# The value product of an attention kernel as three 128-column products in one PSUM bank, in place of a 256- and a 128-column product over two banks

## The chip, the cores and the metric

The kernel runs on one NeuronCore of a Trainium2 chip. A core has a matrix engine (TensorE, PE in the rows, with its weight loads as PEld), VectorE (DVE), ScalarE (ACT), GpSimd (POOL) and a queue engine (SyncE, SP) that issues the transfers. The engines run side by side and wait for each other by semaphores. The metric is the device time of one execution in microseconds, as the median of several runs. A difference of under about 0.5% can't be told from no change here.

## What is computed

One transformer block over x of 8 sequences of 128 tokens and 256 channels, in float32, with 16 heads of 128, followed by a feed-forward stage with ternary weights. The part that matters here is attention:

```
ada = (timestep_embed @ ada_w + ada_b)[:, None, :]
x1 = _ln(x) * (1.0 + scale1) + shift1
qkv = (x1 @ qkv_w + qkv_b).reshape(Bc, Tc, 3, H, DH)
attn = jnp.einsum('bthd,bshd->bhts', q, k) * scale
attn = jax.nn.softmax(attn, axis=-1)
attn_out = jnp.einsum('bhts,bshd->bthd', attn, v).reshape(Bc, Tc, INNER)
attn_out = attn_out @ out_w + out_b
x = x + gate1 * attn_out
...
x = x + gate2 * (h @ ffn_w2 + ffn_b2)          # h = gelu(x2 @ ffn_w1 + ffn_b1)
return x + ternary_ffn(x)                      # relu^2, rms norm, ternary weights
```

## The kernel before

**Split operands.** TensorE multiplies in the format fp32r, which holds less than float32. So every operand is held as two fp32r tiles, a high part and a low part that is the rest, and a product is three: high by high, high by low, low by high, summed in PSUM. `split_mm` (lines 977 to 983) writes these three matmuls for each term. ScalarE makes the high parts out of PSUM (`biased_hi`, `hi_part`), VectorE the low parts (`biased_lo` at line 701, `plain_lo` at line 706): out of the same PSUM bank, it takes the value plus its bias minus the high part.

**Units.** The attention stage is 32 units, numbered i from 0 to 31: four groups of four heads (G), in each of them eight units j, a unit being one head of four sequences. The programs of all engines run over the units in one order, software pipelined: in unit i TensorE computes the scores of unit i (`scores`, 12 products of 128 columns through `split_mm`), transposes the probabilities of unit i-1 (line 1014), projects q and k for unit i+1, multiplies the head output of unit i-2 by the output weights (`out_product`), in four units of each eight also computes two blocks of v (`v_block`), and between these does the value product of unit i-1 (`pv`). Units 0 and 1 stand ahead of a loop over three groups, and the last six units behind it. The order on each engine is written by hand, as is every wait.

**The value product.** `pv(G, j)` waits for the low part of the probabilities (semaphore `p_l`) and for v. For each of the four sequences it takes the 128x128 block v_hi as the stationary operand against the high and the low half of p_split, laid out next to each other, as one product of 256 columns (line 1027), and then v_lo against the high half as one of 128 columns (line 1029), which adds to the first 128 columns of the 256. The result of four sequences takes 4 x 256 columns, that is the two banks of `pv_pair`: `pv_main` is the columns with two of the three terms, `pv_rest` those with the third.

**Its way out.** `o_hi_part` on ScalarE rounds pv_main plus bias to o_hi (semaphore `o_h`). `o_lo_part` on VectorE (lines 714 to 723) takes two instructions: pv_main plus bias minus o_hi into `pv_left` (the tile hbuf, line 720), then, behind a wait for it, pv_rest plus that into o_lo (line 723, semaphore `o_l`). In unit i VectorE does, in this order: the row maximum of the scores (line 779), its scaled copy (line 782), `o_lo_part` of unit i-2, the low part of the probabilities of unit i-1, the reciprocal of the row sums (line 788), the low parts of q and k, and then what the unit has besides. `out_product` of the same unit waits for `o_l`.

**After attention.** The last units also hold the first steps of what follows: transposes of the result (line 1147), the residual add (line 771), its normalisation (lines 654 to 672) and the modulation (line 685). Then come the feed-forward stage with `w1` and `w2` and the ternary stage, which ends the kernel.

Of the kernel before, what the change touches and what calls it, by code (L numbers as in the profile page):

```python
# [14 lines left out]
F32 = mybir.dt.float32  # L15
F32R = mybir.dt.float32r
BF16 = mybir.dt.bfloat16
ALU = mybir.AluOpType
# [3 lines left out]
P = 128  # L22
# [4 lines left out]
HG = 4  # L27
NG = H // HG
SQ = 4
NQ = B // SQ  # L30
TQ = SQ * P
HID = 1024
NC = HID // P
UG = NQ * HG
# [12 lines left out]
QB, KB, VB = NA, NA + H, NA + 2 * H  # L47
# [7 lines left out]
BQ, BK, BV, BS, BO, BY = 0, 1, 2, 3, 4, 6  # L55


def adaln_block(nc, x, cond, ada_w, ada_b, qkv_w, qkv_b, out_w, out_b, ffn_w1, ffn_b1, ffn_w2, ffn_b2,
                w_fc, w_proj, out):
    ctx = ExitStack()  # L60
    with ctx:
        def sb(name, shape, dt=F32):
            return ctx.enter_context(nc.sbuf_tensor(name, shape, dt))

        def sem(name):
            return ctx.enter_context(nc.semaphore(name))
# [24 lines left out]
        v_hi = sb("v_hi", [P, B, HG * P], F32R)  # L91
        v_lo = sb("v_lo", [P, B, HG * P], F32R)
# [5 lines left out]
        p_split = sb("p_split", [P, SQ, 2, P], F32R)  # L98
# [6 lines left out]
        hbuf = sb("hbuf", [P, 2, TQ])  # L105
# [13 lines left out]
        bias = sb("bias", [P, NBIAS])  # L119
# [22 lines left out]
        h2 = raw_qk[:, 0:2, :]  # L142
# [6 lines left out]
                (wo_hi[:, :, :].rearrange("p a b -> p (a b)"), wo_lo[:, :, :].rearrange("p a b -> p (a b)"))))  # L149
        w1T = wqk_hi[:, :, :].rearrange("p a b -> p (a b)")  # L150
        w2T = wqk_lo[:, :, :].rearrange("p a b -> p (a b)")
        pv_left = hbuf[:, 0, :]

        bank = [ctx.enter_context(nc.psum_tensor(f"bank{n}", [P, TQ], F32)) for n in range(BO)]
        pv_pair = ctx.enter_context(nc.psum_tensor("pv_pair", [P, 2 * TQ], F32))
        bank += [pv_pair[:, 0:TQ], pv_pair[:, TQ:2 * TQ]]
        bank += [ctx.enter_context(nc.psum_tensor(f"bank{n}", [P, TQ], F32)) for n in range(BY, 8)]

        pv_main, pv_rest = (pv_pair[:, :].rearrange("p (s x t) -> p s x t", s=SQ, x=2)[:, :, n, :] for n in range(2))


        cond_in, arow_in, bias_in, ada1_in, ada2_in = (
# [16 lines left out]
        q_mm, k_mm, s_mm, t_mm, v_mm, pv_mm, out_mm = (  # L179
            sem(n) for n in ("q_mm", "k_mm", "s_mm", "t_mm", "v_mm", "pv_mm", "out_mm"))  # L180
        q_h, k_h, exp_done, p_h, o_h, v_h = (sem(n) for n in ("q_h", "k_h", "exp_done", "p_h", "o_h", "v_h"))
        o_main = sem("o_main")
        max_done, nb_done, rinv_done, q_l, k_l, p_l, o_l, v_l, y_acc = (
            sem(n) for n in ("max_done", "nb_done", "rinv_done", "q_l", "k_l", "p_l", "o_l", "v_l", "y_acc"))
        norm_done = sem("norm_done")
# [55 lines left out]
        def head_output(i):  # L241

            return (q_hi, q_lo) if isinstance(i, int) and i == NU - 2 else (o_hi, o_lo)
# [57 lines left out]
        def _(pool):  # L301
# [92 lines left out]
            with pool.Fori(0, NG - 1) as G:  # L394
                for g, j, _, _ in group_units(G, range(2, UG + 2)):
                    unit(g, j)
                    if j == 0:
                        ternary_signs(G)
                    if j == 1:
                        ternary_values(G)  # L400
# [24 lines left out]
        def _(act):  # L425
# [32 lines left out]
            def biased_hi(hi, psum, at, ready, count, hi_sem):  # L458
                act.wait_ge(ready, count)
                act.nop(nofuse=True)  # L460
                nc.scalar.activation(hi, psum, ACT.Identity, bias=bias[:, bass.ds(at, 1)]).then_inc(hi_sem, 1)  # L461
# [7 lines left out]
                hi_part(p_split[:, :, 0, :], bank[BV][:, :].rearrange("p (s t) -> p s t", s=SQ), p_h)  # L469

            def o_hi_part(G, j):
                biased_hi(head_output(UG * G + j)[0][:, :].rearrange("p (s t) -> p s t", s=SQ), pv_main, HG * G + VB + j % HG, pv_mm, UG * G + j + 1, o_h)

            def before(G, j):
                return (G, j - 1) if j else (G - 1, UG - 1)
# [11 lines left out]
            def unit(G, j, vs, more, last=False):  # L487
# [50 lines left out]
                if not (isinstance(i, int) and i == 0):  # L538
                    o_hi_part(*before(G, j))
# [31 lines left out]

            modulate(2, SHIFT2, SCALE2, bank[0:2])
            o_hi_part(NG - 1, UG - 1)
            w2_hi_part(3)

# [70 lines left out]
        def _(dve):  # L646
# [29 lines left out]
            def modulate(e, shift, scale, src, between=None):  # L676

                quad = e % NQ
                dve.wait_ge(xt_done, e + 1)
                dve.wait_ge(ada_ready, 1 if e < NQ else 2)  # L680
                if e:
                    dve.wait_ge(xs_lo, KD * e)
                for s in range(SQ):
                    b = quad * SQ + s
                    m = nc.vector.tensor_scalar(xfull[:, 1, s * P:(s + 1) * P], src[1][:, s * P:(s + 1) * P],
                                                ada[:, scale + 1, b:b + 1], ada[:, shift + 1, b:b + 1], ALU.mult, ALU.add)
                m.then_inc(mod_d, 1)
                if between:
                    between()
                dve.wait_ge(mod_d, e + 1)  # L690
                split_lo(quad, KD * e)
# [19 lines left out]
            def p_lo_part(i):  # L711
                plain_lo(p_split[:, :, 1, :], bank[BV][:, :].rearrange("p (s t) -> p s t", s=SQ), p_split[:, :, 0, :], p_h, i + 1, p_l)

            def o_lo_part(G, j, left=pv_left):
                i = UG * G + j
                dve.wait_ge(o_h, i + 1)
                if not isinstance(i, int) or i:
                    dve.wait_ge(o_l, i)
                left, hi, lo = (t.rearrange("p (s t) -> p s t", s=SQ) for t in (left, *(o[:, :] for o in head_output(i))))
                nc.vector.scalar_tensor_tensor(out=left, in0=pv_main, scalar=bias[:, bass.ds(HG * G + VB + j % HG, 1)],  # L720
                                               in1=hi.bitcast(F32), op0=ALU.add, op1=ALU.subtract).then_inc(o_main, 1)
                dve.wait_ge(o_main, i + 1)
                nc.vector.tensor_tensor(lo, pv_rest, left, ALU.add).then_inc(o_l, 1)

            def before(G, j, n):
                return (G, j - n) if j >= n else (G - 1, UG + j - n)
# [33 lines left out]
            def ternary_compare(G, sign):  # L760
                dve.wait_ge(t_thrd, G + 1)
                w = t_bf[:, :].rearrange("p (s c) -> p s c", c=GROUP)
                dst = (t_up if sign > 0 else t_dn)[:, :].rearrange("p (s c) -> p s c", c=GROUP)
                nc.vector.scalar_tensor_tensor(out=dst, in0=w, scalar=float(sign), in1=t_thr[:, :].unsqueeze(2).broadcast_to([P, NS, GROUP]),
                                               op0=ALU.mult, op1=ALU.is_gt).then_inc(t_cmp, 1)
# [9 lines left out]
            def unit(G, j, vs, more, last=False):  # L775
# [7 lines left out]
                if not isinstance(i, int) or i >= 2:  # L783
                    o_lo_part(*before(G, j, 2))
# [60 lines left out]
            for g, j, vs, more in group_units(NG - 1, range(2, UG), last=True):  # L845
                unit(g, j, vs, more, last=True)
            o_lo_part(NG - 1, UG - 2)
            modulate(2, SHIFT2, SCALE2, bank[0:2], lambda: p_lo_part(NU - 1))
            o_lo_part(NG - 1, UG - 1, h2[:, 0, :])
            ternary_compare(NG - 1, -1)  # L850

            def h_lo_part(quad, c):
# [123 lines left out]
        def _(pe):  # L976
            def split_mm(dst, terms, start=True, stop=True):

                for n, (ah, al, bh, bl) in enumerate(terms):
                    nc.tensor.matmul(dst, ah, bh, start=start and n == 0, stop=False)  # L980
                    nc.tensor.matmul(dst, ah, bl, start=False, stop=False)  # L981
                    m = nc.tensor.matmul(dst, al, bh, start=False, stop=stop and n == len(terms) - 1)  # L982
                return m
# [33 lines left out]
            def pv(G, j):  # L1017
                a, quad = j % HG, j // HG
                pe.wait_ge(p_l, UG * G + j + 1)
                if isinstance(G, int) and UG * G + j == NU - 2:  # L1020
                    pe.wait_ge(o_l, NU - 2)
                pe.wait_ge(v_l, UG * G + SQ * (quad + 1))
                for s in range(SQ):
                    b, h = quad * SQ + s, slice(a * P, (a + 1) * P)
                    at = 2 * s * P

                    nc.tensor.matmul(pv_pair[:, at:at + 2 * P], v_hi[:, b, h], p_split[:, s, :, :].rearrange("p x t -> p (x t)"),  # L1027
                                     start=True, stop=False)
                    m = nc.tensor.matmul(pv_pair[:, at:at + P], v_lo[:, b, h], p_split[:, s, 0, :], start=False, stop=True)  # L1029
                m.then_inc(pv_mm, 1)  # L1030

            def out_product(G, j):
# [14 lines left out]
            def unit(G, j, vs, more, extra=None):  # L1047
# [13 lines left out]
                if known and i == NU - 1:  # L1061
                    transpose_xr(0, bank[0:2])
                    out_product(*before(G, j, 2))
                    pv(*before(G, j, 1))
                    pe.wait_ge(p_l, i)
                    transpose_p(i, j % 2)
                    pe.wait_ge(xrT_done, 1)
                    transpose_x(2, bank[0:2])
                    return
# [8 lines left out]
                if not known or i >= 1:  # L1078
                    pv(*before(G, j, 1))
# [7 lines left out]
            for k in range(KD):  # L1087
                m = nc.tensor.transpose(bank[7][:, k * B:(k + 1) * B], crow[:, k * P:(k + 1) * P], ident[0:B, 0:B])
# [244 lines left out]
```

## Time and profile before

| | us |
|---|---|
| median of 3 runs | 390.71 |
| lowest and highest | 390.7 and 392.43 |
| span of the profiled execution | 391.2 |

| engine | busy us | share of the span |
|---|---|---|
| PE | 367.8 | 94% |
| PEld | 319.5 | 82% |
| DVE | 288.0 | 74% |
| ACT | 237.0 | 61% |
| POOL | 129.7 | 33% |

Times in the rows are microseconds from the start of the profiled execution, except means, which are nanoseconds. Matmuls are pipelined: the end of one is modelled, and overlaps the start of the next, so that what a matmul costs in a dense stretch is the distance from its start to the start of the next one, and not its duration. Idle time of an engine is listed in front of the instruction that it waited for, with the engine and line that ended it.

### The profile page before, as it was taken

Reading aid. Unit: us, or ns where it says so; the run is one execution under the profiler, and the core shown is the slowest. Engines: PE = TensorE matmul, PEld = TensorE weight load, DVE = VectorE, ACT = ScalarE, POOL = GpSimd, SP = SyncE. Lnnn points to the kernel's source line nnn. Section 1 sums busy time; section 2 is a strip of 40 time slices with the busy share of each in tenths; the row PEclk is TensorE's granted clock in tenths of the full one; section 3 lists DMA queues with packets and bytes.
Section 4 is the critical chain, followed back from the end, with each engine's and each line's share of the span. In section 5 each row is a group of like instructions: output and inputs, shape, how many; then the busy total and the mean of one; then the engine's idle time right before and its main releaser. Section 6 shows DMA issues by size and latency. Waiting matters only on the chain. (4 is left out here: it accounts for less than half of the span.)

```text
span 391.2 us, 6260 instructions
## 1 busy us (share of the span) xinstructions
PE 367.8 (94%) x2096; PEld 319.5 (82%) x2096; DVE 288.0 (74%) x486; ACT 237.0 (61%) x582; POOL 129.7 (33%) x111
## 2 busy tenths in 40 slices
PE   2899999999999999999999999999889899996975
PEld 2789888888888888888888898889778787885855
DVE  5775569768776976866887667689988638797793
ACT  1464576665666566656676566775687358573751
POOL 1522224321542232272323144335423300162451
PEclk9999999999999999999999999999999999998995
DMA  7913031000303100030200012010000000000002
GB/s 231 358 61 108 1 109 54 2 0 3 108 0 107 54 0 0 0 107 29 78 0 0 0 26 83 0 55 1 2 0 1 2 0 2 0 1 2 8 19 80
DMA packets 11778, 16.53 MB, mean 42 GB/s; under 512 B 672, under 2 KB 7920, under 8 KB 11760
## 3 DMA queue, kind: packets, MB, share of 16 engines
q1 hardware_dynamic: 11760, 16.30, 12.6%
q8 instruction: 10, 0.16, 0.2%
q14 instruction: 8, 0.07, 0.1%
HBM read 15.25 MB, written 1.05 MB: 42 GB/s over the span
## 5 line engine op out<-in xcount | busy, mean ns | idle before, releaser
L345 POOL TENSOR_TENSOR prob<-prob,rinv 128x512 f32<-128x512 f32 x32 | 33.4, 1043 | 152.4 <-DVE rinv L788 152.4
L980 PE MATMUL bank<-x_hi,wqk_hi 128*128 128x512 f32 x128 | 54.4, 425 | 0.0
L982 PE MATMUL bank<-x_hi,wqk_lo 128*128 128x512 f32 x128 | 51.3, 401 | 0.0
L981 PE MATMUL bank<-x_lo,wqk_hi 128*128 128x512 f32 x128 | 51.1, 399 | 0.0
L706 DVE TENSOR_TENSOR v_lo<-bank,v_hi 128x512 fp32r<-128x512 f32 x30 | 20.7, 691 | 39.2 <-ACT v_hi L427 39.2
L493 ACT ACTIVATE prob<-bank,nbias 128x128 f32<-128x128 f32 x128 | 45.1, 370 | 4.1 <-DVE nbias L782 4.1
L427 ACT ACTIVATE p_split<-bank 128x512 fp32r<-128x512 f32 x32 | 19.1, 598 | 35.4 <-PE bank L1014 35.4
L461 ACT ACTIVATE o_hi<-pv_pair,bias 128x512 fp32r<-128x512 f32 x31 | 21.3, 688 | 24.3 <-PE pv_pair L1029 24.3
L982 PE MATMUL bank<-k_hi,q_lo 128*128 128x128 f32 x128 | 35.4, 276 | 0.0
L417 POOL TENSOR_TENSOR raw_qk<-raw_qk 128x512 f32<-128x512 f32 x13 | 18.4, 1415 | 50.7 <-ACT raw_qk L622 50.4
L981 PE MATMUL bank<-k_lo,q_hi 128*128 128x128 f32 x128 | 35.2, 275 | 0.0
L980 PE MATMUL bank<-k_hi,q_hi 128*128 128x128 f32 x128 | 34.3, 268 | 0.0
L1027 PE MATMUL pv_pair<-p_split,v_hi 128*128 128x256 f32 x128 | 31.4, 323 | 0.4 <-DVE xr L771 0.2
L427 ACT ACTIVATE v_hi<-bank 128x512 fp32r<-128x512 f32 x30 | 17.9, 596 | 22.7 <-PE bank L982 22.5
L779 DVE TENSOR_REDUCE negmax<-bank 128x4 f32<-128x512 f32 x32 | 22.1, 690 | 11.0 <-PE bank L982 11.0
L982 PEld LDWEIGHTS bank<-x_hi,wqk_lo 128*128 128x128 f32 x128 | 24.8, 193 | 5.9
L701 DVE SCALAR_TENSOR_TENSOR k_lo<-bank,bias,k_hi 128x512 fp32r<-128x512 f32 x32 | 24.0, 749 | 7.0 <-ACT k_hi L461 7.0
L981 PEld LDWEIGHTS bank<-x_lo,wqk_hi 128*128 128x128 f32 x128 | 24.9, 195 | 4.4
L1029 PE MATMUL pv_pair<-p_split,v_lo 128*128 128x128 f32 x128 | 28.5, 222 | 0.0
L980 PEld LDWEIGHTS bank<-x_hi,wqk_hi 128*128 128x128 f32 x128 | 24.9, 194 | 4.1
L701 DVE SCALAR_TENSOR_TENSOR q_lo<-bank,bias,q_hi 128x512 fp32r<-128x512 f32 x32 | 24.0, 751 | 5.0 <-ACT q_hi L461 3.4
L461 ACT ACTIVATE k_hi<-bank,bias 128x512 fp32r<-128x512 f32 x32 | 22.2, 692 | 8.6 <-PE bank L982 8.6
(206 smaller groups left out, 1086.9 us busy)
## 6 DMA issues: line engine op xcount, KB each, us to landing
raw_qk<-in_L_cond_qkv_w_dram SPq DMA_DIRECT2D x8, 512.0 KB, 4.9
raw_v<-in_L_cond_qkv_w_dram SPq DMA_DIRECT2D x4, 512.0 KB, 3.8
raw_o<-in_L_cond_out_w_dram SPq DMA_DIRECT2D x4, 512.0 KB, 3.6
xt<-in_x_dram SPq DMA_DIRECT2D x2, 512.0 KB, 5.0
xr<-in_L_cond_ada_w_dram SPq DMA_DIRECT2D x1, 1024.0 KB, 10.2
raw_w<-in_L_cond_ffn_w_dram SPq DMA_DIRECT2D x2, 512.0 KB, 7.6
t_raw<-in_L_ffn_W_fc_dram SPq DMA_DIRECT2D x4, 256.0 KB, 3.8
t_raw<-in_L_ffn_W_proj_dram SPq DMA_DIRECT2D x4, 256.0 KB, 3.9
```

Source lines behind the costliest of these rows:

```text
L345: nc.gpsimd.tensor_tensor(e, e, rinv[:, j % 2, :].unsqueeze(2).broadcast_to([P, SQ, P]), ALU.mult).then_inc(norm_done, 1)
L427: nc.scalar.activation(hi, raw, ACT.Copy).then_inc(hi_sem, 1)
L461: nc.scalar.activation(hi, psum, ACT.Identity, bias=bias[:, bass.ds(at, 1)]).then_inc(hi_sem, 1)
L493: e = nc.scalar.activation(prob[:, j % 2, s, :], bank[BS][:, s * P:(s + 1) * P], ACT.Exp, bias=nbias[:, j % 2, s:s + 1], scale=SCALE, accu ...
L701: nc.vector.scalar_tensor_tensor(out=lo[:, :], in0=psum[:, :], scalar=bias[:, bass.ds(at, 1)], in1=hi[:, :].bitcast(F32), op0=ALU.add, op1 ...
L706: nc.vector.tensor_tensor(lo, psum, hi.bitcast(F32), ALU.subtract).then_inc(lo_sem, 1)
L779: nc.vector.tensor_reduce(negmax[:, j % 2, :], bank[BS][:, :].rearrange("p (s t) -> p s t", s=SQ), axis=AX.X, op=ALU.max, negate=True).the ...
L980: nc.tensor.matmul(dst, ah, bh, start=start and n == 0, stop=False)
L981: nc.tensor.matmul(dst, ah, bl, start=False, stop=False)
L982: m = nc.tensor.matmul(dst, al, bh, start=False, stop=stop and n == len(terms) - 1)
L1027: nc.tensor.matmul(pv_pair[:, at:at + 2 * P], v_hi[:, b, h], p_split[:, s, :, :].rearrange("p x t -> p (x t)"), start=True, stop=False)
L1029: m = nc.tensor.matmul(pv_pair[:, at:at + P], v_lo[:, b, h], p_split[:, s, 0, :], start=False, stop=True)
```

## The change

The value product is written with `split_mm`, as the scores are: for each sequence v_hi by p_hi, v_hi by p_lo and v_lo by p_hi, each of 128 columns, all three into the same 128 columns of one bank. `pv_pair`, its two halves and the buffer `pv_left` are gone, the banks 4 and 5 are separate ones, and `o_lo_part` is one call of `biased_lo`, with one instruction. The waits for `o_main` and for the preceding `o_l` go with the second instruction. Nothing else changes.

```diff
-        pv_pair = ctx.enter_context(nc.psum_tensor("pv_pair", [P, 2 * TQ], F32))
-        bank += [pv_pair[:, 0:TQ], pv_pair[:, TQ:2 * TQ]]
...
-        pv_main, pv_rest = (pv_pair[:, :].rearrange("p (s x t) -> p s x t", s=SQ, x=2)[:, :, n, :] for n in range(2))
+        bank = [ctx.enter_context(nc.psum_tensor(f"bank{n}", [P, TQ], F32)) for n in range(8)]
...
             def o_hi_part(G, j):
-                biased_hi(head_output(UG * G + j)[0][:, :].rearrange("p (s t) -> p s t", s=SQ), pv_main, HG * G + VB + j % HG, pv_mm, UG * G + j + 1, o_h)
+                biased_hi(head_output(UG * G + j)[0][:, :], bank[BO][:, :], HG * G + VB + j % HG, pv_mm, UG * G + j + 1, o_h)
...
-            def o_lo_part(G, j, left=pv_left):
-                i = UG * G + j
-                dve.wait_ge(o_h, i + 1)
-                if not isinstance(i, int) or i:
-                    dve.wait_ge(o_l, i)
-                left, hi, lo = (t.rearrange("p (s t) -> p s t", s=SQ) for t in (left, *(o[:, :] for o in head_output(i))))
-                nc.vector.scalar_tensor_tensor(out=left, in0=pv_main, scalar=bias[:, bass.ds(HG * G + VB + j % HG, 1)],
-                                               in1=hi.bitcast(F32), op0=ALU.add, op1=ALU.subtract).then_inc(o_main, 1)
-                dve.wait_ge(o_main, i + 1)
-                nc.vector.tensor_tensor(lo, pv_rest, left, ALU.add).then_inc(o_l, 1)
+            def o_lo_part(G, j):
+                hi, lo = head_output(UG * G + j)
+                biased_lo(lo, bank[BO], HG * G + VB + j % HG, hi, o_h, UG * G + j + 1, o_l)
...
-                    at = 2 * s * P
-
-                    nc.tensor.matmul(pv_pair[:, at:at + 2 * P], v_hi[:, b, h], p_split[:, s, :, :].rearrange("p x t -> p (x t)"),
-                                     start=True, stop=False)
-                    m = nc.tensor.matmul(pv_pair[:, at:at + P], v_lo[:, b, h], p_split[:, s, 0, :], start=False, stop=True)
+                    m = split_mm(bank[BO][:, s * P:(s + 1) * P], [(v_hi[:, b, h], v_lo[:, b, h], p_split[:, s, 0, :], p_split[:, s, 1, :])])
```

How instructions stand in a row, first on TensorE in the loop: the value product of unit i-1, between the output product (o_hi, o_lo against wo) and the scores of the next unit. Before:

```order
L982 MATMUL bank<-o_hi,wo_lo 128x512
L1027 MATMUL pv_pair<-p_split,v_hi 128x256
L1029 MATMUL pv_pair<-p_split,v_lo 128x128
L1027 MATMUL pv_pair<-p_split,v_hi 128x256
L1029 MATMUL pv_pair<-p_split,v_lo 128x128
...
L980 MATMUL bank<-k_hi,q_hi 128x128
L981 MATMUL bank<-k_lo,q_hi 128x128
```

In the changed kernel `split_mm` has the lines 966 to 968:

```order
L968 MATMUL bank<-o_hi,wo_lo 128x512
L966 MATMUL bank<-p_split,v_hi 128x128
L967 MATMUL bank<-p_split,v_hi 128x128
L968 MATMUL bank<-p_split,v_lo 128x128
L966 MATMUL bank<-p_split,v_hi 128x128
L967 MATMUL bank<-p_split,v_hi 128x128
L968 MATMUL bank<-p_split,v_lo 128x128
...
L966 MATMUL bank<-k_hi,q_hi 128x128
L967 MATMUL bank<-k_lo,q_hi 128x128
```

Eight matmuls have become twelve, in the same place; each brings a weight load of its own. The second place is VectorE in unit 31, the last one, from the row maximum to the modulation (xfull) that follows attention. Before:

```order
L779 TENSOR_REDUCE negmax<-bank 128x4
L782 TENSOR_SCALAR nbias<-negmax 128x4
L720 SCALAR_TENSOR_TENSOR hbuf<-pv_pair,bias,o_hi 128x512
L723 TENSOR_TENSOR o_lo<-pv_pair,hbuf 128x512
L706 TENSOR_TENSOR p_split<-bank,p_split 128x4x128
L788 RECIPROCAL rinv<-rowsum 128x4
L672 TENSOR_SCALAR raw_qk<-xr,mv,rstd 128x256 x4
L720 SCALAR_TENSOR_TENSOR hbuf<-pv_pair,bias,q_hi 128x512
L723 TENSOR_TENSOR q_lo<-pv_pair,hbuf 128x512
L685 TENSOR_SCALAR xfull<-bank,ada 128x128 x4
```

In the changed kernel:

```order
L765 TENSOR_REDUCE negmax<-bank 128x4
L768 TENSOR_SCALAR nbias<-negmax 128x4
L694 SCALAR_TENSOR_TENSOR o_lo<-bank,bias,o_hi 128x512
L699 TENSOR_TENSOR p_split<-bank,p_split 128x4x128
L774 RECIPROCAL rinv<-rowsum 128x4
L665 TENSOR_SCALAR raw_qk<-xr,mv,rstd 128x256 x4
L694 SCALAR_TENSOR_TENSOR q_lo<-bank,bias,q_hi 128x512
L678 TENSOR_SCALAR xfull<-bank,ada 128x128 x4
```

The second instruction of each o_lo is gone (the pair on q_lo is that of unit 30, whose head output lies in q_hi and q_lo), and all that follows it on VectorE has moved up by one place; no instruction has changed its order.

## Rows read from the trace of the kernel before

**Rows 1.** The page: its head, and busy us (share of the span) xinstructions.
```profile
span 391.2 us, 6260 instructions
...
PE 367.8 (94%) x2096; PEld 319.5 (82%) x2096; DVE 288.0 (74%) x486; ACT 237.0 (61%) x582; POOL 129.7 (33%) x111
```
**Rows 2.** Busy time by stretch (PE, PEld, DVE, ACT, POOL; PEclk, DMA share, GB/s).
```profile
43.00:275.00 232.00, 232.00 (x1372) 204.04 (x1371) 172.84 (x292) 148.96 (x406) 81.62 (x65) 1.00 0.11 34
275.00:291.00 16.00, 13.52 (x90) 11.22 (x88) 14.85 (x34) 12.03 (x31) 5.88 (x6) 1.00 0.00 1
...
338.00:391.00 53.00, 42.04 (x230) 36.65 (x228) 40.31 (x49) 28.14 (x52) 21.55 (x16) 0.88 0.06 20
```
**Rows 3.** Groups by line, 43 to 275 us, PE (busy us, mean ns, idle before).
```profile
L982 PE MATMUL bank<-k_hi,q_lo 128*128 128x128 f32 x116 | 32.0, 276 | 0.0
...
L1027 PE MATMUL pv_pair<-p_split,v_hi 128*128 128x256 f32 x116 | 28.3, 322 | 0.0
```
**Rows 4.** Groups by line, 43 to 275 us, DVE.
```profile
L720 DVE SCALAR_TENSOR_TENSOR hbuf<-pv_pair,bias,o_hi 128x512 f32<-128x512 f32 x29 | 21.7, 749 | 0.6
...
L723 DVE TENSOR_TENSOR o_lo<-pv_pair,hbuf 128x512 fp32r<-128x512 f32 x29 | 20.0, 691 | 1.0
```
**Rows 5.** Timeline, PE, a unit with v blocks (start, duration, engine, line, xcount).
```profile
108.30 0.28 PE L1027 MATMUL pv_pair<-p_split,v_hi 128*128 128x256 f32 x1
...
109.17 0.45 PE L980 MATMUL bank<-wv_hi,x_hi 128*128 128x512 f32 x1
...
110.60 0.22 PE L980 MATMUL bank<-k_hi,q_hi 128*128 128x128 f32 x1
...
111.89 0.62 PE L1014 MATMUL bank<-ident,prob 128*128 128x128 f32 x4
```
**Rows 6.** Timeline, PE, scores that follow a value product directly.
```profile
101.01 0.28 PE L980 MATMUL bank<-k_hi,q_hi 128*128 128x128 f32 x1
...
102.35 0.63 PE L1014 MATMUL bank<-ident,prob 128*128 128x128 f32 x4
```
**Rows 7.** Timeline, PE, eight 128-column products with bf16 operands.
```profile
324.12 0.62 PE L1213 MATMUL bank<-ident_bf,t_w 128*128 128x128 bf16 x8
324.55 0.48 PE L980 MATMUL bank<-x_hi,w_hi 128*128 128x512 f32 x1
```
**Rows 8.** The page: costliest groups, ScalarE on two banks and on one.
```profile
L461 ACT ACTIVATE o_hi<-pv_pair,bias 128x512 fp32r<-128x512 f32 x31 | 21.3, 688 | 24.3 <-PE pv_pair L1029 24.3
...
L461 ACT ACTIVATE k_hi<-bank,bias 128x512 fp32r<-128x512 f32 x32 | 22.2, 692 | 8.6 <-PE bank L982 8.6
```
**Rows 9.** Timeline, DVE, two instructions of the form that the change leaves.
```profile
269.36 0.75 DVE L701 SCALAR_TENSOR_TENSOR q_lo<-bank,bias,q_hi 128x512 fp32r<-128x512 f32 x1
270.02 0.74 DVE L701 SCALAR_TENSOR_TENSOR k_lo<-bank,bias,k_hi 128x512 fp32r<-128x512 f32 x1
```
**Rows 10.** Timeline, DVE, units 31 and after ([idle before <-releaser]).
```profile
281.69 0.75 DVE L720 SCALAR_TENSOR_TENSOR hbuf<-pv_pair,bias,o_hi 128x512 f32<-128x512 f32 x1
282.48 0.69 DVE L723 TENSOR_TENSOR o_lo<-pv_pair,hbuf 128x512 fp32r<-128x512 f32 x1
283.08 0.68 DVE L706 TENSOR_TENSOR p_split<-bank,p_split 128x512 fp32r<-128x512 f32 x1
...
286.59 0.75 DVE L720 SCALAR_TENSOR_TENSOR hbuf<-pv_pair,bias,q_hi 128x512 f32<-128x512 f32 x1 [0.75 <-ACT q_hi L461]
```
**Rows 11.** Timeline, PE, where it waits near the end of attention.
```profile
278.37 0.39 PE L1027 MATMUL pv_pair<-p_split,v_hi 128*128 128x256 f32 x1 [0.22 <-DVE xr L771]
...
283.22 0.50 PE L980 MATMUL bank<-o_hi,wo_hi 128*128 128x512 f32 x1 [1.04 <-DVE o_lo L723]
...
288.12 0.50 PE L980 MATMUL bank<-q_hi,wo_hi 128*128 128x512 f32 x1 [1.03 <-DVE q_lo L723]
...
289.99 0.39 PE L1027 MATMUL pv_pair<-p_split,v_hi 128*128 128x256 f32 x1 [0.20 <-DVE p_split L706]
...
291.19 0.50 PE L980 MATMUL bank<-x_hi,w_hi 128*128 128x512 f32 x1
```

More of the change, by code:

```diff
@@ L151, in adaln_block @@
         w2T = wqk_lo[:, :, :].rearrange("p a b -> p (a b)")
-        pv_left = hbuf[:, 0, :]
-        bank = [ctx.enter_context(nc.psum_tensor(f"bank{n}", [P, TQ], F32)) for n in range(BO)]
-        pv_pair = ctx.enter_context(nc.psum_tensor("pv_pair", [P, 2 * TQ], F32))
-        bank += [pv_pair[:, 0:TQ], pv_pair[:, TQ:2 * TQ]]
-        bank += [ctx.enter_context(nc.psum_tensor(f"bank{n}", [P, TQ], F32)) for n in range(BY, 8)]
-        pv_main, pv_rest = (pv_pair[:, :].rearrange("p (s x t) -> p s x t", s=SQ, x=2)[:, :, n, :] for n in range(2))
+        bank = [ctx.enter_context(nc.psum_tensor(f"bank{n}", [P, TQ], F32)) for n in range(8)]
         cond_in, arow_in, bias_in, ada1_in, ada2_in = (
@@ L181, in adaln_block @@
         q_h, k_h, exp_done, p_h, o_h, v_h = (sem(n) for n in ("q_h", "k_h", "exp_done", "p_h", "o_h", "v_h"))
-        o_main = sem("o_main")
         max_done, nb_done, rinv_done, q_l, k_l, p_l, o_l, v_l, y_acc = (
@@ L848, in _ @@
             modulate(2, SHIFT2, SCALE2, bank[0:2], lambda: p_lo_part(NU - 1))
-            o_lo_part(NG - 1, UG - 1, h2[:, 0, :])
+            o_lo_part(NG - 1, UG - 1)
             ternary_compare(NG - 1, -1)
```

## Prediction

> **What bounds the kernel now.** The head of the page comes first [rows 1]: TensorE is busy for 94% of the span, VectorE for 74%. That is an average, so the next view is the busy time by stretch [rows 2]. From 43 to 275 us, which holds 29 of the 32 value products (116 of the 256-column matmuls, four to a block, [rows 3]), TensorE is busy for 232.00 of 232.00 us at the full granted clock, and VectorE for 172.84. From 275 to 291 us it is the other way round: VectorE 14.85 of 16, TensorE 13.52. In the last stretch neither is full, and the work there (the ternary stage) isn't touched.
>
> The groups by line say the same from the side of the waits: in the long stretch the idle time before the value product and before the scores is 0.0 [rows 3]. VectorE is never late for TensorE there. Only near the end of attention does TensorE stand and wait for VectorE, four times, and two of these waits, of 1.04 and 1.03 us, are for the second instruction of o_lo [rows 11]. So the change takes work from an engine that has slack in 232 of 391 us, and the question is what it adds to the one that has none.
>
> **What a value product costs on TensorE.** A busy PE says nothing of its price, since the rows overlap; starts do. Before, a block of four sequences runs from 108.30 to 109.17, when the next product starts: 0.87 us for 8 matmuls [rows 5], about 0.11 us for each, whether it has 256 or 128 columns. The new block is 12 matmuls of 128 columns through the same helper as the scores, with operands of the same type and size, of which the first two share their stationary operand. So the scores are the price of the new block. After a 512-column product, as the value product also comes, the 12 matmuls of the scores run from 110.60 to 111.89: 1.29 us [rows 5]. After a value product, whose last matmul is a short one, they run from 101.01 to 102.35: 1.34 us [rows 6]. I take 1.29, since a value product follows a 512-column one in the order of both kernels, and keep 1.34 for the upper end. The price of a block is 1.29 - 0.87 = **0.42 us**, up to 0.47.
>
> That it is the number of weight loads that costs and not the columns can be seen twice. Both forms stream 4 x 384 columns, and yet 12 matmuls take half as long again as 8. And with bf16 operands eight products of 128 columns take 324.55 - 324.12 = 0.43 us, 0.054 each [rows 7], half of the 0.11 of the fp32r ones: neither the columns nor the issue of instructions holds the latter. There are as many loads as matmuls, 2096 of each [rows 1], so a load isn't left out where two products in a row have the same weights.
>
> The Trainium skill, "TensorE: Matmul & The Clock Gate", section "Back-to-back issue gap", gives for an isolated stream 134 cycles at 128 columns and 262 at 256, some 56 and 109 ns; by it a block would cost 4 x (109 + 56) = 0.66 us before and 12 x 56 = 0.67 after, that is nothing more. The same section's sustained 81 ns for 128 columns would make the new block 0.97 us and the difference 0.10 us a unit, 3 us in all. Its section on LDWEIGHTS, 128 columns / 1.2 = 107 ns, is the one near the rows here, and four loads more by it are 0.43 us.
>
> **TensorE in the long stretch.** 29 blocks x 0.42 = **+12.2 us** (29 x 0.47 = 13.6 at most). All of it is on the path, since there is no idle time in front of any of them.
>
> **What VectorE saves.** Before, o_lo is two instructions, 749 and 691 ns [rows 4]; from the start of the first to the start of what follows the second it takes 283.08 - 281.69 = 1.39 us [rows 10]. After, it is one of the form of q_lo, whose successor starts 270.02 - 269.36 = 0.66 us later [rows 9]. So 0.73 us a unit go, 23 us of busy time over 32 units. In the long stretch they go into VectorE's idle time and bring nothing: TensorE waits for no VectorE result there. The output on one bank in place of two costs ScalarE the same: 688 ns for o_hi, 692 for k_hi out of one bank [rows 8]. Nothing moves past a queue, no wait is added, and no transfer or GpSimd instruction changes: no cost.
>
> **The end of attention.** Here the 0.73 us counts, against three more blocks (29, 30, 31) of 0.42. I walk it relative to the shift that the 29 blocks have made. Block 29 waits for the residual add (278.37, [rows 11]). VectorE comes to this add some 0.7 us earlier but then has to wait for TensorE's transposes, so the block starts only 0.2 us earlier, and with its 0.42 the scores behind it start 0.1 to 0.2 us later than before. Then o_lo of unit 29 is ready about 0.6 us earlier (one instruction instead of two, from a start 0.1 us later), and the output product, which waited 1.04 us for it, starts at about -0.6. Block 30 takes that to -0.2. The next o_hi is bound by ScalarE and comes 0.1 us later, so o_lo starts at 286.7 and is ready at 287.4 instead of 288.1 [rows 10, 11]: the output product starts at -0.65. Block 31 waits behind the modulation for p_lo, which is earlier by the same amount, and with its 0.42 the feed-forward stage starts at about **-0.3 us** against 291.19. From -1 to +0.5 seems possible, as three waits change owner here.
>
> **Behind it.** The feed-forward and ternary stages have the same instructions. What can change is where the low clock falls: from 338 us on the mean granted clock is 0.88 of full [rows 2], and TensorE isn't full there. I count 0, with 1 us to either side.
>
> **Sum.** 12.2 - 0.3 = +11.9 us on the span of 391.2, which gives 403.1. The median of the runs, 390.7, is 0.5 below the profiled span, so I forecast 402.6 us, 3% slower. From the terms' ends: 390.7 + 11.9 - 0.7 - 1 = 400.9 and 390.7 + 13.6 + 0.5 + 1 = 405.8.
>
> **Rivals.** (A) Not slower: the price is in the columns, or the second load of v_hi comes for free, so that a block still costs 0.87 us. What speaks for it: the array streams the same 1536 columns. Then only the end of attention changes: the two waits of 1.04 and 1.03 us for o_lo lose up to 0.7 each, 390.7 - 1.4 = 389.3 us. If short products even ran at the bf16 pace of 0.054 us, a block would be 12 x 0.054 = 0.65 us, 29 x 0.22 = 6.4 us less, near 383 us. It decides from a spacing of below 0.073 us a matmul (0.87 / 12). Against it: the scores' 0.11 us in every unit. The skill's table of isolated gaps, named above, is this rival. (B) A smaller loss: TensorE's unbroken busy time hides short waits for VectorE of under 0.2 us that the overlap of the rows covers, and VectorE's freed 0.73 us takes them away. With 0.1 to 0.2 us in each of 29 units, 3 to 6 us come back: 396.6 to 399.7 us. Against it: the starts inside and around the blocks are evenly spaced. (C) A larger loss: in the half of the units without v blocks the new block stands directly in front of the scores, and 12 + 12 + 4 short products follow each other where it was 8 + 12 + 4. If TensorE's supply of instructions falls behind there by 0.22 us, the shortest idle time that it has in these rows [rows 11], 15 units pay 3.3 us more: 405.9 us. Against it: 12 + 4 in a row run at 0.11 us without a gap.
>
> **Chances.** Forecast (400 to 405.5) 0.84; A 0.05, of which 0.03 at 389 and 0.02 below; B 0.06; C 0.05. Taken together the range is 400.0 to 405.4 us. The bound of 0.5% lies at 388.8 and 392.7 us: faster 0.02, the same 0.03, slower 0.95.
>
> **What would show it.** In the changed kernel's rows: starts of the value product's matmuls 0.11 us apart and a block of 1.29 us (A: 0.87 or less); loads and matmuls 2096 + 128 = 2224 of each; VectorE busy for some 22 us less, near 266, and TensorE still without idle time to the end of unit 28; the waits of 1.04 and 1.03 us for o_lo down to 0.3 to 0.6. If the loop's units grow by clearly less than 0.42 us with blocks of 1.29, it is B, if there are gaps inside a run of short products, C. The forecast is wrong above all if the scores are no fair model of the new block: their operands come from tiles of 512 columns, those of the value product from v_hi with 4096 and from the interleaved halves of p_split.

## The result and the profile after

| | before | changed |
|---|---|---|
| median us | 390.7 (4 runs) | 402.92 (4 runs) |
| lowest and highest | 390.65 and 392.43 | 402.21 and 404.13 |
| ratio, 95% interval | | 1.0295 [1.0258, 1.0332] |
| span of the profiled execution | 391.2 | 400.7 |

The change makes the kernel 12.2 us slower, against a forecast of 11.9. The spans of the two profiled executions differ by 9.5 us only; that gap is taken up below.

The head of the page, and busy time by stretch (PE, PEld, DVE, ACT, POOL, then PEclk), of the changed kernel. They answer to [rows 1] and [rows 2]:

```profile
span 400.7 us, 6452 instructions
...
PE 378.9 (95%) x2224; PEld 331.2 (83%) x2224; DVE 268.3 (67%) x454; ACT 236.8 (59%) x582; POOL 129.5 (32%) x111
```
```profile
43.00:285.00 242.00, 242.00 (x1473) 214.26 (x1472) 154.21 (x262) 148.33 (x406) 80.23 (x64) 1.00 0.10 33
285.00:301.00 16.00, 15.20 (x103) 12.73 (x102) 13.00 (x30) 11.45 (x29) 5.82 (x6) 1.00 0.00 0
```

TensorE has 128 matmuls and 128 loads more and is still busy without a gap from 43 to 285 us. VectorE has 32 instructions and 19.7 us less to do (288.0 to 268.3), all of which it now spends waiting. The value product on TensorE in a unit without v blocks, and its start behind a v block, which answer to [rows 5] and [rows 6]:

```profile
100.83 0.22 PE L966 MATMUL bank<-p_split,v_hi 128*128 128x128 f32 x1
100.89 0.28 PE L967 MATMUL bank<-p_split,v_hi 128*128 128x128 f32 x1
101.00 0.27 PE L968 MATMUL bank<-p_split,v_lo 128*128 128x128 f32 x1
...
102.12 0.28 PE L966 MATMUL bank<-k_hi,q_hi 128*128 128x128 f32 x1
...
103.46 0.40 PE L1000 MATMUL bank<-ident,prob 128*128 128x128 f32 x2
```
```profile
109.41 0.22 PE L966 MATMUL bank<-p_split,v_hi 128*128 128x128 f32 x1
...
110.70 0.45 PE L966 MATMUL bank<-wv_hi,x_hi 128*128 128x512 f32 x1
```

A block takes 102.12 - 100.83 = 1.29 us, or 110.70 - 109.41 = 1.29, where it took 0.87. The scores behind it take 103.46 - 102.12 = 1.34, as before. The weight loads (PEld) start 0.11 us apart as well, each at about the time at which the product ahead of its own starts:

```profile
100.84 0.19 PEld L967 LDWEIGHTS bank<-p_split,v_hi 128*128 128x128 f32 x1
100.95 0.19 PEld L968 LDWEIGHTS bank<-p_split,v_lo 128*128 128x128 f32 x1
```

To measure the whole long stretch free of what happens at either end, take the start of the scores of unit 2 and of unit 30. In the kernel before:

```profile
45.23 0.22 PE L980 MATMUL bank<-k_hi,q_hi 128*128 128x128 f32 x1
...
271.15 0.28 PE L980 MATMUL bank<-k_hi,q_hi 128*128 128x128 f32 x1
```

In the changed one:

```profile
43.43 0.22 PE L966 MATMUL bank<-k_hi,q_hi 128*128 128x128 f32 x1
...
281.10 0.28 PE L966 MATMUL bank<-k_hi,q_hi 128*128 128x128 f32 x1
```

225.92 us have become 237.67: +11.75, or 0.42 for each of the 28 blocks between (units 2 to 29, with the value products of units 1 to 28). These two starts are the yardstick for the experiments too; below they are "the 28 units".

### The profile page after: what moved, and what is told of

Same layout as the page of the kernel before. It is cut to its first block and busy times, and to the rows that moved or that the text cites. A ratio compares the mean times of both kernels' runs of the same rounds, so it can differ in the third digit from the quotient of the medians.

```text
span 400.7 us, 6452 instructions
## 1 busy us (share of the span) xinstructions
PE 378.9 (95%) x2224; PEld 331.2 (83%) x2224; DVE 268.3 (67%) x454; ACT 236.8 (59%) x582; POOL 129.5 (32%) x111
## 3 DMA queue, kind: packets, MB, share of 16 engines
q1 hardware_dynamic: 11760, 16.30, 12.2%
## 5 line engine op out<-in xcount | busy, mean ns | idle before, releaser
L966 PE MATMUL bank<-x_hi,wqk_hi 128*128 128x512 f32 x128 | 53.2, 415 | 0.0
L699 DVE TENSOR_TENSOR v_lo<-bank,v_hi 128x512 fp32r<-128x512 f32 x32 | 22.1, 691 | 45.8 <-ACT v_hi L420 45.8
L968 PE MATMUL bank<-x_hi,wqk_lo 128*128 128x512 f32 x128 | 50.3, 393 | 0.0
L967 PE MATMUL bank<-x_lo,wqk_hi 128*128 128x512 f32 x128 | 49.8, 389 | 0.0
L454 ACT ACTIVATE o_hi<-bank,bias 128x512 fp32r<-128x512 f32 x31 | 21.3, 688 | 36.6 <-PE bank L968 36.6
L968 PE MATMUL bank<-p_split,v_lo 128*128 128x128 f32 x128 | 35.3, 276 | 0.0
L967 PE MATMUL bank<-p_split,v_hi 128*128 128x128 f32 x128 | 35.2, 275 | 0.0
L966 PE MATMUL bank<-p_split,v_hi 128*128 128x128 f32 x128 | 33.6, 262 | 0.2 <-DVE p_split L699 0.2
L420 ACT ACTIVATE v_hi<-bank 128x512 fp32r<-128x512 f32 x32 | 19.2, 599 | 23.3 <-PE bank L968 23.2
```

The lines of the kernel that those rows point to most:

```text
L420: nc.scalar.activation(hi, raw, ACT.Copy).then_inc(hi_sem, 1)
L699: nc.vector.tensor_tensor(lo, psum, hi.bitcast(F32), ALU.subtract).then_inc(lo_sem, 1)
```

## The experiments

The theory is that of the prediction: an fp32r product of 128 or of 256 columns costs what its weight load costs, 0.11 us, so the price is in the number of products; VectorE's relief counts at the end of attention only. The rivals are that the adding of three products into one bank costs, that columns cost, that VectorE's lateness was hidden in every unit, and that the cost can be had back by another order. Every kernel is compared with the kernel before on the same chip; its median was 392.03 (29 runs) in the comparison with e1, e2, e3 and e6, and 391.08 (17 runs) in that with the others. The expectations give their times from a kernel before of 390.7, so what can be held against them is the difference.

| kernel | products in a block, columns in all | banks, o_lo instructions | median us | ratio to before | 28 units us | block us |
|---|---|---|---|---|---|---|
| before | 8, 1536 | 2, 2 | 390.7 | 1 | 225.92 | 0.87 |
| changed | 12, 1536 | 1, 1 | 402.92 | 1.0295 [1.0258, 1.0332] | 237.67 | 1.29 |
| e1 | 12, 1536 | 2, 2 | 404.82 | 1.0333 [1.0296, 1.0369] | 237.68 | 1.29 |
| e2 | 8, 1536 | 2, 1 | 390.63 | 0.9971 [0.9946, 0.9995] | 225.71 | 0.87 |
| e3 | 8, 2048 | 2, 2 | 392.65 | 1.0021 [0.9999, 1.0044] | 226.50 | 0.95 |
| e6 | 8, 1024 | 1, 1 | 390.71 | 0.997 [0.9945, 0.9996] | 225.19 | 0.84 |
| changed, again | 12, 1536 | 1, 1 | 403.43 | 1.0302 [1.0272, 1.0333] | 237.67 | 1.29 |
| e5 | 12, 1536 | 1, 1 | 404.77 | 1.0348 [1.0318, 1.0378] | 238.21 | 2.68 with the output product |
| e7 | 8, in two units 12 | 2, 2 and 1, 1 | 391.02 | 0.999 [0.9966, 1.0014] | 226.00 | 0.87, in two units 1.29 |

The start of what follows a block is drawn up to 0.06 us earlier or later by whether a wide or a narrow product stands last, so the 28 units are the better measure of a price than one block.

### e1: twelve products, but two banks and two VectorE instructions

```diff
-                    nc.tensor.matmul(pv_pair[:, at:at + 2 * P], v_hi[:, b, h], p_split[:, s, :, :].rearrange("p x t -> p (x t)"),
-                                     start=True, stop=False)
+                    nc.tensor.matmul(pv_pair[:, at + P:at + 2 * P], v_hi[:, b, h], p_split[:, s, 1, :], start=True, stop=True)
+                    nc.tensor.matmul(pv_pair[:, at:at + P], v_hi[:, b, h], p_split[:, s, 0, :], start=True, stop=False)
```

> The kernel before, with its 256-column product cut into two of 128 columns (p_lo into its half of the pair first, then p_hi); both banks, both VectorE instructions of o_lo and all waits stay. Theory (a weight load costs 0.11 us whether its product has 128 or 256 columns): blocks of 1.29 us, 29 x 0.42 = +12.2 us, and since VectorE is not relieved the last three blocks cost too, +0.5 to +1.3: 403.4 to 404.2 us. Rival (the three terms in one bank, adding to the same 128 columns, are what costs): blocks stay near 0.87 us and the time near 391 us.

Measured: 404.82 us, 12.8 more than before, where the expectation had 12.7 to 13.5 (403.4 to 404.2 less 390.7). The 28 units take 237.68 us, to 0.01 those of the changed kernel. So the whole cost in the long stretch comes from cutting the wide product in two, and the single bank has no part in it. At the end of attention TensorE waits for VectorE as in [rows 11]:

```profile
295.02 0.50 PE L980 MATMUL bank<-o_hi,wo_hi 128*128 128x512 f32 x1 [1.04 <-DVE o_lo L723]
...
300.32 0.50 PE L980 MATMUL bank<-q_hi,wo_hi 128*128 128x512 f32 x1 [1.02 <-DVE q_lo L723]
```

From the scores of unit 30 (282.76) to the first product of the feed-forward stage (303.58) it is 20.82 us, in the changed kernel 300.80 - 281.10 = 19.70. The difference, 1.12 us, is what the changed kernel gains by its shorter o_lo.

### e2: one VectorE instruction, TensorE untouched

```diff
...
-                nc.vector.scalar_tensor_tensor(out=left, in0=pv_main, scalar=bias[:, bass.ds(HG * G + VB + j % HG, 1)],
-                                               in1=hi.bitcast(F32), op0=ALU.add, op1=ALU.subtract).then_inc(o_main, 1)
-                dve.wait_ge(o_main, i + 1)
-                nc.vector.tensor_tensor(lo, pv_rest, left, ALU.add).then_inc(o_l, 1)
+                nc.vector.scalar_tensor_tensor(out=lo, in0=pv_main, scalar=bias[:, bass.ds(HG * G + VB + j % HG, 1)],
+                                               in1=hi.bitcast(F32), op0=ALU.add, op1=ALU.subtract).then_inc(o_l, 1)
```

> The kernel before, with TensorE untouched and o_lo as one VectorE instruction: the second one, which adds v_hi by p_lo, is left out, so that term is missing from the output. It prices VectorE's relief by itself. Theory (the relief counts at the end of attention alone): the waits of 1.04 and 1.03 us shrink to 0.3 to 0.4, 389.0 to 390.0 us. Rival (TensorE's unbroken busy time hides short waits for VectorE in every unit): 3 to 6 us less, 385 to 388 us.

Measured: 390.63 us against 392.03, 0.9971 [0.9946, 0.9995]; the 1.4 us less are in what was expected (0.7 to 1.7), though the time itself isn't, since the kernel before took 392.03 there. The 28 units shrink by 0.21 us of 225.92, where the rival asked for 3 to 6. Of the 0.21, 0.18 are hidden waits of the rival's kind after all: three units (4, 12 and 20) of the kernel before last 6.86 us, the others of their form 6.80, as all of them do here. No such wait stands on TensorE's matmul rows, but one stands on its weight loads, in front of the output product, in the kernel before:

```profile
65.99 0.19 PEld L980 LDWEIGHTS bank<-o_hi,wo_hi 128*128 128x128 f32 x1 [0.20 <-DVE o_lo L723]
```

The page shows VectorE at 268.8 us in place of 288.0: 19 us of work taken from an engine, and in the trace about 1 us of time, 0.21 in the 28 units, 0.54 at the end of attention, where 20.04 us become 19.50, and 0.25 behind it. TensorE's waits there, as in [rows 11], with VectorE's relief:

```profile
280.48 0.50 PE L976 MATMUL bank<-o_hi,wo_hi 128*128 128x512 f32 x1 [0.31 <-DVE o_lo L718]
283.91 1.07 PE L1102 MATMUL bank<-ident,raw_qk 128*128 128x128 f32 x8 [0.46 <-DVE raw_qk L672]
285.23 0.50 PE L976 MATMUL bank<-q_hi,wo_hi 128*128 128x512 f32 x1 [0.25 <-DVE q_lo L718]
...
288.64 0.50 PE L976 MATMUL bank<-x_hi,w_hi 128*128 128x512 f32 x1 [0.40 <-DVE x_lo L696]
```

The two waits of 1.04 and 1.03 us did shrink to 0.31 and 0.25. But two others have come up, 0.46 for the normalised x and 0.40 for the low part of the modulated one, which were hidden behind them. That is why 1.5 us less of waiting for o_lo is worth 0.54. In the changed kernel, whose blocks are longer, less of these two shows (the transposes of the normalised x start 0.21 us later behind those ahead of them than before, and no listed wait is for x_lo), and the same relief is worth the 1.12 us found with e1.

### e3 and e6: eight products, all wide or all narrow

e3, in the kernel before:

```diff
-                    m = nc.tensor.matmul(pv_pair[:, at:at + P], v_lo[:, b, h], p_split[:, s, 0, :], start=False, stop=True)
+                    m = nc.tensor.matmul(pv_pair[:, at:at + 2 * P], v_lo[:, b, h], p_split[:, s, :, :].rearrange("p x t -> p (x t)"),
+                                         start=False, stop=True)
```

> The kernel before, with v_lo against both halves of p, so that all eight products of a block have 256 columns (2048 columns in place of 1536; a fourth term is added to the output). Theory (loads set the price): a block of 0.87 to 0.92 us, 391 to 392.3 us. Rival (columns set it): 0.87 x 2048 / 1536 = 1.16 us a block, +8.4 us, 399 us.

e6, in the changed kernel:

```diff
-                    m = split_mm(bank[BO][:, s * P:(s + 1) * P], [(v_hi[:, b, h], v_lo[:, b, h], p_split[:, s, 0, :], p_split[:, s, 1, :])])
+                    at = bank[BO][:, s * P:(s + 1) * P]
+                    nc.tensor.matmul(at, v_hi[:, b, h], p_split[:, s, 0, :], start=True, stop=False)
+                    m = nc.tensor.matmul(at, v_hi[:, b, h], p_split[:, s, 1, :], start=False, stop=True)
```

> The changed kernel without its third term (v_lo by p_hi is left out of the output): eight products of 128 columns a block, 1024 columns, one bank, one VectorE instruction. Theory (loads set the price): a block of 0.85 us, as before the change with half as many columns again, 389 to 390 us. Rival (columns): 0.87 x 1024 / 1536 = 0.58 us a block, -8.4 us, 381 us. A spacing between means that the weights of two products in a row, which are the same here in all of them, are in part loaded for free.

Measured: 392.65 and 390.71 us, that is 0.6 more and 1.3 less than before, near the theory and far from the rival (+8.4 and -8.4). A block of e3 takes 0.95 us, a little above the 0.87 to 0.92 expected. Starts of the products in e3, all of 256 columns:

```profile
97.64 0.28 PE L1027 MATMUL pv_pair<-p_split,v_hi 128*128 128x256 f32 x1
97.76 0.28 PE L1029 MATMUL pv_pair<-p_split,v_lo 128*128 128x256 f32 x1
97.88 0.28 PE L1027 MATMUL pv_pair<-p_split,v_hi 128*128 128x256 f32 x1
...
98.59 0.22 PE L980 MATMUL bank<-k_hi,q_hi 128*128 128x128 f32 x1
```

And in e6, all of 128:

```profile
98.25 0.28 PE L1013 MATMUL bank<-p_split,v_hi 128*128 128x128 f32 x1
98.36 0.27 PE L1012 MATMUL bank<-p_split,v_hi 128*128 128x128 f32 x1
98.47 0.27 PE L1013 MATMUL bank<-p_split,v_hi 128*128 128x128 f32 x1
...
99.03 0.28 PE L966 MATMUL bank<-k_hi,q_hi 128*128 128x128 f32 x1
```

0.12 us from start to start with 256 columns, 0.11 with 128. Over the 28 units, twice as many columns (e3 against e6) cost 226.50 - 225.19 = 1.31 us, 0.05 a unit, of which 0.21 in all is VectorE's, by e2; four products more of the same size (the changed kernel against e6) cost 237.67 - 225.19 = 12.48 us, 0.45 a unit, 0.11 for each. Columns up to 256 are nearly free, products aren't. The rival by columns, with 399 and 381 us, is out. In e6 the two products of a sequence have the same weights throughout, and keep the spacing of 0.11: nothing is saved on a load that repeats the one before.

What these runs show is a price for each product. That it is the price of its weight load is the reading that fits them, with the loads' starts 0.11 us apart; no run changes the load and leaves the product. One row of the kernel before fits it too, 16 products of only 8 columns (their weights are plain float32):

```profile
33.69 1.84 PE L1097 MATMUL bank<-condT,xr 128*128 128x8 f32 x16
35.39 0.31 PE L980 MATMUL bank<-k_hi,q_hi 128*128 128x128 f32 x1
```

From the first to what follows it is 1.70 us, 0.106 for each.

### e5: the short products between long ones

If loads are the price and a 512-column product takes twice the 0.11 us at which loads follow each other (0.227), the spare time could be under the long products. The edit, in the changed kernel, in the units without v blocks:

```diff
...
+                for k in range(6):
+                    c, x, y, n = long[k]
+                    w = (wo_hi, wo_lo)[x][:, a, c * P:(c + 1) * P]
+                    ml = nc.tensor.matmul(bank[BY + c][:, :], w, y[:, :], start=a == 0 and n == 0, stop=a == HG - 1 and n == 2)
+                    for s, m3 in short[2 * k:2 * k + 2]:
...
+                        ms_ = nc.tensor.matmul(bank[BO][:, s * P:(s + 1) * P], (v_hi, v_hi, v_lo)[m3][:, b, h],
+                                               p_split[:, s, (0, 1, 0)[m3], :], start=m3 == 0, stop=m3 == 2)
```

> The changed kernel, where in the units without v blocks the twelve 128-column products of the value product stand between the six 512-column ones of the output product: one long, two short, one long, two short, and so on; both waits come ahead of the first. Nothing else changes. Theory (a load runs under the one product ahead of it and no further): a pair of short ones after a long one costs two loads more, as before, so the joined block takes 6 x 0.227 + 12 x 0.11 = 2.7 us and the time is the changed kernel's, within 0.5%. Rival (loads run ahead under a long product by more than one): columns set the pace, 6 x 0.227 + 12 x 0.056 = 2.03 us, 0.6 us less in each of some 14 units, 394 us.

Measured: 404.77 us, 1.0348 [1.0318, 1.0378], against 403.43 us, 1.0302 [1.0272, 1.0333], for the changed kernel run beside it, for which this was expected:

> The changed kernel once more, on the same chip as the two that follow. Ratio to the kernel before 1.029 to 1.033.

The joined block, L1029 being the long products:

```profile
99.44 0.39 PE L1029 MATMUL bank<-o_hi,wo_hi 128*128 128x512 f32 x1
99.67 0.33 PE L1032 MATMUL bank<-p_split,v_hi 128*128 128x128 f32 x2
99.83 0.45 PE L1029 MATMUL bank<-o_lo,wo_hi 128*128 128x512 f32 x1
100.12 0.22 PE L1032 MATMUL bank<-p_split,v_lo 128*128 128x128 f32 x1
100.18 0.27 PE L1032 MATMUL bank<-p_split,v_hi 128*128 128x128 f32 x1
100.29 0.45 PE L1029 MATMUL bank<-o_hi,wo_lo 128*128 128x512 f32 x1
...
102.12 0.28 PE L966 MATMUL bank<-k_hi,q_hi 128*128 128x128 f32 x1
```

And its loads:

```profile
99.89 0.19 PEld L1032 LDWEIGHTS bank<-p_split,v_lo 128*128 128x128 f32 x1
100.12 0.19 PEld L1032 LDWEIGHTS bank<-p_split,v_hi 128*128 128x128 f32 x1
```

One long and two short ones take 100.29 - 99.83 = 0.46 us, and the block 102.12 - 99.44 = 2.68, where six long ones and then twelve short ones take 6 x 0.227 + 1.29 = 2.65. The loads fit this: that of the first short product is done at 100.08, under the long one, and that of the second doesn't start before the first short product does, at 100.12. So in these runs a load is hidden under no more than the one product ahead of it, and the spare time under a long product can't be collected for two short ones. The time is even a little worse: the 28 units take 0.54 us more than the changed kernel's, and the end of attention 0.72 more (20.42 against 19.70). There, in unit 29, the output product ends only with the joined block, and VectorE, which adds it up, starts later by that; the delay goes on to the residual add and from there to the value product in unit 30, which isn't joined:

```profile
281.52 1.41 DVE L721 SCALAR_TENSOR_TENSOR yT<-bank,bias,yT 128x512 f32<-128x512 f32 x2 [0.98 <-PE bank L1029]
289.21 0.33 PE L966 MATMUL bank<-p_split,v_hi 128*128 128x128 f32 x1 [0.74 <-DVE xr L757]
```

The rival, 394 us, is out.

### e7: the changed form where TensorE waits, and only there

The result of e2 and the changed kernel's waits suggest a version between the two: pairs in units 0 to 28 and 31, one bank in 29 and 30.

```diff
+        def one_bank(i):
+            return isinstance(i, int) and i in (NU - 3, NU - 2)
...
+                if one_bank(i):
+                    hi, lo = head_output(i)
+                    return biased_lo(lo, bank[BO], HG * G + VB + j % HG, hi, o_h, i + 1, o_l)
...
+                    if one_bank(UG * G + j):
+                        m = split_mm(bank[BO][:, s * P:(s + 1) * P], [(v_hi[:, b, h], v_lo[:, b, h], p_split[:, s, 0, :], p_split[:, s, 1, :])])
+                        continue
```

> The kernel before, with the changed form (three 128-column products into one bank, one VectorE instruction) in units 29 and 30 alone, where TensorE waits for o_lo. Theory: the two waits of 1.04 and 1.03 us shrink by 0.7 each, two blocks cost 0.42 more, net -0.4 to -0.8 us against the kernel before, 0.1 to 0.2% less, which the ratio can hardly tell from 1; the waits in the profile tell. Rival (the relief is worth nothing at the end either, since another wait takes its place): +0.4 to +0.8 us.

Measured: 391.02 us against 391.08, 0.999 [0.9966, 1.0014]. The expected gain is missed. Its waits:

```profile
282.29 0.50 PE L988 MATMUL bank<-o_hi,wo_hi 128*128 128x512 f32 x1 [0.30 <-DVE o_lo L706]
...
287.05 0.50 PE L988 MATMUL bank<-q_hi,wo_hi 128*128 128x512 f32 x1 [0.25 <-DVE q_lo L706]
...
290.46 0.50 PE L988 MATMUL bank<-x_hi,w_hi 128*128 128x512 f32 x1 [0.40 <-DVE x_lo L701]
```

The waits for o_lo went as expected, 1.5 us of them. Two blocks took 0.84 of that. The transposes of the normalised x start 0.22 us later behind those ahead of them than before, and at the entry of the feed-forward stage, where the listed wait is 0.40 for x_lo, the last block and what follows it take 1.54 us in place of 1.20. From the scores of unit 30 (270.54) to that entry it is 19.92 us, 0.12 less than before: theory and rival each had half of it. No version here that computes all three terms beats the kernel before by more than a measurement can tell.

## Why the prediction was right, step by step

**The bound.** TensorE without a gap through the attention stage, VectorE with slack: confirmed after the change by the busy times above and by e2, where 19 us less work on VectorE moved the 28 units by 0.21 us. "VectorE is never late for TensorE there" was a little too strong: it is, by 0.06 us in three units. Nor is the end of attention the only other place where TensorE waits for it: the trace before has 1.21 us for v_lo at 310.63, in the feed-forward stage, and 3.9 and 2.9 us in all for two low parts in the ternary stage. None of these is for o_lo.

**The price of a block.** 0.42 us taken from the scores, 0.42 measured, in the changed kernel and in e1. The step that could have failed was to take the scores as the model of a block with other operands; they were a fair one. That the price is by products and not by columns, which the prediction read from two places in the trace, is shown by e3 and e6; that it is the loads' stays a reading. The table of isolated spacings in the Trainium skill ("TensorE: Matmul & The Clock Gate", section "Back-to-back issue gap"), which would have made the change free on TensorE, doesn't hold for this stream: it gives 56 ns for 128 columns, and e6 and the changed kernel show 0.11 us.

**The sum.** 28 blocks of +11.75 in all and the first one, whose distance from its start to the scores of unit 2 grew from 2.30 to 2.73 us, make 12.2, the number of the sum.

**The end of attention.** Forecast -0.3 against the shift of the 29 blocks. Measured from the scores of unit 30 (271.15 and 281.10) to the feed-forward stage (291.19 and 300.80): 20.04 and 19.70 us, -0.34. The walk holds at each step: from the scores of unit 30 the scores of unit 31 come 0.19 us later than before (forecast 0.1 to 0.2), the first output product behind them 0.55 earlier (0.6), the second 0.68 earlier (0.65). The waits of 1.04 and 1.03 us for o_lo, named as going down to 0.3 to 0.6, are 0.30 and 0.25:

```profile
292.62 0.50 PE L966 MATMUL bank<-o_hi,wo_hi 128*128 128x512 f32 x1 [0.30 <-DVE o_lo L694]
```

On VectorE the step from o_lo to what follows, 1.39 us in [rows 10], is 292.49 - 291.82 = 0.67, for which 0.66 was taken:

```profile
291.82 0.74 DVE L694 SCALAR_TENSOR_TENSOR o_lo<-bank,bias,o_hi 128x512 fp32r<-128x512 f32 x1
292.49 0.68 DVE L699 TENSOR_TENSOR p_split<-bank,p_split 128x512 fp32r<-128x512 f32 x1
293.51 0.18 DVE L774 RECIPROCAL rinv<-rowsum 128x4 f32<-128x4 f32 x1 [0.34 <-ACT prob L486]
```

The last row has a wait for ScalarE's exponentials that the walk didn't name and for which TensorE has no wait listed. The bound that it did name, ScalarE's o_hi of unit 30, is there; forecast 0.1 us later than before, relative to the scores of unit 30 the instruction behind it starts 0.04 later:

```profile
296.58 0.75 DVE L694 SCALAR_TENSOR_TENSOR q_lo<-bank,bias,q_hi 128x512 fp32r<-128x512 f32 x1 [0.65 <-ACT q_hi L454]
```

**What was mis-sized.** Two terms, both small. VectorE's relief was called 23 us of busy time, near 266 us after; it was 19.7, 268.3 us, or 0.62 an instruction. The 0.73 was a distance between starts: 0.04 of it was idle time (281.69 + 0.75 to 282.48, [rows 10]), and about 0.08 comes back where the reciprocal, which followed p_split directly, now waits and overlaps nothing. And rival A's price for the relief without the blocks, 1.4 us, was too high: e2's trace has 0.54 at the end of attention, since two waits that the prediction didn't look for take over there. The median of e2 says 1.4 less, with an interval (0.2 to 2.1 us) that holds both.

**What stood on a weak footing.** The prediction added 11.9 to the median, by way of a profiled span 0.5 above it. That relation was not typical. Each timed execution here whose span is listed lies 1.75 us or more above its span (402.52 and 400.7 in the changed kernel), so the profiled execution of the kernel before was a long one. It has a stretch at half clock in its start, and the changed one hasn't. Busy time from 38 to 41 us, before and changed (the value behind POOL's is PEclk):

```profile
38.00:41.00 3.00, 3.00 (x9) 2.41 (x8) 1.15 (x3) 2.10 (x10) 1.04 (x1) 0.54 0.00 0
```
```profile
38.00:41.00 3.00, 3.00 (x17) 2.53 (x15) 1.72 (x4) 2.67 (x9) 1.16 (x2) 1.00 0.00 0
```

With the first products 0.6 us earlier as well, the changed kernel reaches the scores of unit 2 at 43.43 instead of 45.23 + 0.43. That is 2.2 of the 2.7 us by which the spans differ less than the medians; 0.1 is behind attention, and the rest is the 12.2 of the medians against the 11.8 of the trace. The changed kernel run again bears it out: in that trace the clock does fall (0.68 from 38 to 41 us), the scores of unit 2 start at 45.18, the span is 402.0, and the 28 units take 237.67 us as before. The sum was right as a difference. As an absolute time it owes something to luck: the span of a long execution happened to lie only 0.5 us above the median, so that 402.6 and 403.1 were both near.

**The rivals.** B (hidden waits) is worth 0.18 us and not 3 to 6. The argument against it, that the starts are evenly spaced, was a misreading; in the kernel before they alternate between 0.06 and 0.17 to 0.18 us, as behind [rows 5]:

```profile
108.42 0.22 PE L1029 MATMUL pv_pair<-p_split,v_lo 128*128 128x128 f32 x1
108.47 0.34 PE L1027 MATMUL pv_pair<-p_split,v_hi 128*128 128x256 f32 x1
108.65 0.22 PE L1029 MATMUL pv_pair<-p_split,v_lo 128*128 128x128 f32 x1
```

It was e2 that settled it. C (gaps in long runs of short products) has nothing for it: 12 + 12 short products run at 0.11 us without a gap. Its price was read with 0.22 us as the shortest wait, where [rows 11] has 0.20; that makes 3.0 us and not 3.3. Units with and without v blocks grew by 0.41 to 0.47 us, but for the three with the hidden wait, which grew by 0.36.

## What to carry to other kernels

Count the matmuls, not their columns, where the operands are fp32r and the products 128 or 256 columns wide: here each costs 0.11 to 0.12 us, the distance at which weight loads follow each other, so laying two moving operands next to each other and doing one wide product saves a whole one, and is worth a second bank and 0.7 us on another engine as long as that engine has slack. Price a change on a dense engine by the distance between starts of the same form elsewhere in the trace, and an engine's relief only by the waits that end on it; for TensorE look for them on the rows of its weight loads as well, where waits show that the matmul rows cover. Before counting on such a relief, look at what else arrives just behind the wait that goes.

## What the hardware showed that wasn't expected

- 128-column products placed in pairs between 512-column ones cost their full 0.11 us each (0.46 for one long and two short, e5), though the long product takes 0.227 us, twice as much.
- In four of the nine traces (before, the changed kernel again, e1, e7) TensorE's clock falls to its lower level, 1.2 GHz of 2.4, for some 3 us around 37 to 40.5 us (mean granted clock from 38 to 41 us: 0.54, 0.68, 0.67, 0.72); in the other five it stays at 1.00 over the same instructions. TensorE wasn't idle ahead of it: before, it was busy for 3.00 of the 3.00 us from 34 to 37, first with products of 8 columns (16 of them from 33.69 to 35.39), then with the 12 scores of unit 1 and four transposes. The stretch from the scores of unit 1 to the first value product took 7.5 us with the low clock (35.39 to 42.93) and 5.95 without (34.75 to 40.70). Runs of the kernel before differ by up to 3.5 us (390.11 to 393.66); how much of that is this isn't shown.
